# Routed-expert stage of a four-layer block: the normalisation of groups 2 to 7 moves from VectorE to ScalarE, and the last statistics move around the first group

## The chip, the cores and the metric

The kernel runs on one core of one Trainium2 chip. The metric is the device time of one execution in microseconds. A core has a matrix engine (TensorE, PE in the profile), VectorE (DVE), ScalarE (ACT), GpSimd (POOL) and SyncE (SP), which run their own instruction streams and meet at semaphores. An engine takes its own instructions strictly in the order in which they are written.

## The reference, cut to what matters

Eight residual sublayers run one after the other on x of 16 x 256 tokens by 128 features, in float32. Before each stands a layer norm of every token. The fourth is a routed mixture of 16 small experts with the best four chosen per token:

```python
def _layernorm(x, axis=-1, eps=1e-05):
    m = jnp.mean(x, axis=axis, keepdims=True)
    v = jnp.var(x, axis=axis, keepdims=True)
    return (x - m) / jnp.sqrt(v + eps)

def _L1_ffn_ref(x, expert_sel, keys, values, route_scale):     # 16 experts of width 32, K = 4
    sel_probs = jax.nn.sigmoid(jnp.einsum('btd,ed->bte', x, expert_sel))
    _, sel_index = jax.lax.top_k(sel_probs, K)
    sel_val = jnp.take_along_axis(sel_probs, sel_index, axis=-1)
    sel_val = sel_val / jnp.clip(sel_val.sum(-1, keepdims=True), 1e-09) * route_scale
    scores_all = jax.nn.relu(jnp.einsum('btd,edh->bteh', x, keys))
    values_all = jnp.einsum('bteh,ehv->btev', scores_all, values)
    selected = jnp.take_along_axis(values_all, sel_index[..., None], axis=2)
    return (selected * sel_val[..., None]).sum(axis=2)

x = x + _L0_xattn_ref(...); x = x + _L0_ffn_ref(...)
x = x + _L1_xattn_ref(_layernorm(x), ...)      # attention "a1"
x = x + _L1_ffn_ref(_layernorm(x), ...)        # routed experts "f1": the changed stage
x = x + _L2_xattn_ref(...); x = x + _L2_ffn_ref(...); x = x + _L3_xattn_ref(...); x = x + _L3_ffn_ref(...)
```

## The kernel before

**Layout.** X stays in on-chip memory for the whole kernel, as 32 tiles of 128 tokens by 128 features. Four tiles are a group, so there are 8 groups. The sublayers are named a0, f0, a1, f1, a2, f2, a3, f3. There is no scheduler and no planner: each engine has one function per sublayer, and the order of the work on an engine is the order of the Python code, written by hand. Semaphores counted from the start of the kernel tie the engines together.

**The layer norm** is made in pieces. When a residual has been added to a group (residual, L295), VectorE takes the statistics of its four tiles (BN_STATS, L302). Mean and variance are worked out for a stretch of tiles at once: ln_var_dve is six small VectorE operations (L217 to L225), ln_finish_act is two on ScalarE, Ln and Exp, which give one over the root of the variance (L255, L257), and ln_rstd_dve is four on VectorE (L236 to L242). For f1 the tiles are in two parts, tiles 0 to 23 (part 0, groups 0 to 5) and tiles 24 to 31 (part 1, groups 6 and 7): EARLY is 24. Part 0 is done inside the attention a1. Then a group is normalised into hrow, one of two buffers, in four operations of 128x128, by VectorE (normalise, L271, subtract and multiply) or by ScalarE (normalise_act, L264, Identity with scale and bias). TensorE turns the four tiles by transposes (turn, L282), and ScalarE copies the result into hT (take_turned, L287).

**The stage f1** handles group g in body(g, ...) on TensorE, ScalarE and VectorE. On TensorE body g does, in this order:

- turn(g+1), which waits until group g+1 is normalised;
- for g from 1 to 6 a piece of the next attention a2: its keys K (L471, which for g = 2, 3 and 4 wait for VectorE's operations on the piece before), then its values V (L339);
- keys(0), keys(1) (L1518), tr(0) (L1525), keys(2), tr(1), the routing logits of group g+1 (L1471), val(0) (L1535), keys(3), tr(2), val(1), tr(3), val(2), val(3).

Here keys(t) multiplies tile t by all experts' keys, tr(t) transposes the hidden values, and val(t) multiplies them by the values. Between them VectorE makes hidden(t) (L1639, relu times gate) and ScalarE hidT(t) (L1600, the copy of the transposed hidden values, for which val(t) waits). In the words below, hidT(t) is ScalarE's operation L1600 for tile t. VectorE's body g does hidden(0), hidden(1), the residual of group g-1, hidden(2), hidden(3), the gates of group g+1 (f1_gates, L1484 to L1501), **the normalisation of group g+2 (L271)**, and then small pieces for a2: masks at g = 0 (L770), keys_cos at g = 1 (L748), keys_sin at g = 2 (L754 to L759), keys16 and keys_cos at g = 3 (L765, L748), keys_sin at g = 4, keys16 at g = 5. At g = 0 the whole finish of part 1 (L217 to L242, with ScalarE's L255 and L257 in the middle) stands between the gates and the normalisation. VectorE starts the stage with `dve.sem_inc(S("f1_hid"), 2)` (L1632), for which TensorE's keys(0) of group 0 waits.

Of the kernel before, what the change touches and what calls it, by code (L numbers as in the profile page):

```python
# [30 lines left out]
N_GROUPS = N_TILES // 4  # L31
# [40 lines left out]
def build(nc, dram):  # L72
    with ExitStack() as ctx:
# [66 lines left out]
        def bank(i):  # L140
            return psum[:, i, :]
# [25 lines left out]
        EARLY = 24  # L167
# [7 lines left out]
        def ln_parts(s):  # L175
            return LN_PARTS.get(s, ((0, N_TILES),))
# [8 lines left out]
        def sem(s, name):  # L185
            return S("all_" + name)

        def at(s, name):
            return sum(count(x, name) for x in SUB[:SUB.index(s)])
# [55 lines left out]
        def ln_finish_dve(dve, s, k=0):  # L245
            ln_var_dve(dve, s, k)
            ln_rstd_dve(dve, s, k)

        def ln_finish_act(act, s, k=0):

            lo, hi = ln_parts(s)[k]
            if s in ("a0", "a1") and k == 0:
                act.preload_act_table_set("natural_log_exp_and_others")
            act.wait_ge(sem(s, "var"), at(s, "var") + k + 1)
            act.activation(lnw[:, 5, lo:hi], lnw[:, 4, lo:hi], ACT.Ln).then_inc(S("all_lnv"), 1)  # L255
            act.wait_ge(S("all_lnv"), at(s, "var") + k + 1)
            act.activation(lnw[:, 6, lo:hi], lnw[:, 5, lo:hi], ACT.Exp, scale=-0.5).then_inc(sem(s, "std"), 1)  # L257

        def normalise_act(act, s, g, j, k=0):
            act.wait_ge(sem(s, "ln"), at(s, "ln") + LN_STEPS * (k + 1))  # L260
            act.wait_ge(sem(s, "normed"), at(s, "normed") + g)
            act.wait_ge(sem(s, "turned"), at(s, "turned") + g + 1)
            for t in range(GT):
                ins = act.activation(hrow[:, j, t * P:(t + 1) * P], tile_of(X, 4 * g + t), ACT.Identity,  # L264
                                     scale=rstd[:, ds(4 * g + t, 1)], bias=shifted[:, ds(4 * g + t, 1)])
            ins.then_inc(sem(s, "normed"), 1)

        def normalise(dve, s, g, j):
            dve.wait_ge(sem(s, "turned"), at(s, "turned") + g + 1)
            for t in range(GT):  # L270
                ins = dve.tensor_scalar(hrow[:, j, t * P:(t + 1) * P], tile_of(X, 4 * g + t),  # L271
                                        mean[:, ds(4 * g + t, 1)], rstd[:, ds(4 * g + t, 1)],
                                        ALU.subtract, ALU.mult)
            ins.then_inc(sem(s, "normed"), 1)
# [32 lines left out]
        def stats_done(dve, s, nxt, k=0):  # L307
            dve.wait_ge(sem(s, "bn"), at(s, "bn") + ln_parts(nxt)[k][1])
            dve.sem_inc(sem(nxt, "stats"), 1)
# [489 lines left out]
        def heads_dve(dve, L, o, nxt):  # L799
            s = L.s  # L800
            early = nxt.early
            mx, norm, res = o.mx, o.norm, o.res
            for b in range(B + 2):
                if b + 2 < B:
                    mx(b + 2, 0)
                    mx(b + 2, 1)
                if b == 1:
                    ln_rstd_dve(dve, s, 1)
                if 1 <= b <= B:
                    norm(b - 1)  # L810
                if b == B - 2 and early:
                    ln_rstd_dve(dve, nxt.s, 0)
                    normalise(dve, nxt.s, 0, 0)
                if b == B and early:
                    nxt.gates0(dve)
                if b >= 2 and b % 2:
                    res((b - 3) // 2)
                if b == B - 3 and early:
                    stats_done(dve, s, nxt.s, 0)
                    ln_var_dve(dve, nxt.s, 0)  # L820
            stats_done(dve, s, nxt.s, int(early))

# [630 lines left out]
        f1 = Carve()  # L1455
# [19 lines left out]
        def f1_exps(act, g, j):  # L1475

            act.wait_ge(S("f1_lg"), g + 1)
            act.activation(prob1[j], bank(1)[:, 0:GT * MOE1_E], ACT.Exp, scale=-1.0).then_inc(S("f1_ex"), 1)
# [111 lines left out]
        def f1_act(act, a2):  # L1590
            act.sem_inc(S("f1_hidT"), 2)

            def body(g, j, last):
                if not last:
                    take_turned(act, "f1", g + 1, 1 - j)
                for t in range(GT):
                    act.wait_ge(S("f1_tr"), 4 * g + t + 1)
                    if t >= 2:
                        act.wait_ge(S("f1_val"), 4 * g + t - 1)
                    act.activation(hidT1[t % 2], bank(4 + t % 2), ACT.Copy).then_inc(S("f1_hidT"), 1)  # L1600
                    if t == 1 and not last:
                        f1_exps(act, g + 1, 1 - j)
                    if t == 1 and last:
                        take_turned(act, "a2", 0, 0)
                    if t >= 2 and last:
                        a2.takeQ(t - 2)
                    if t == 0 and g in (5, 6):
                        a2.values(2 * g - 10, 6)
                    if t == 0 and last:
                        normalise_act(act, "a2", 1, 1)  # L1610
                if g == 3:
                    a2.keys16(0)
                if g == 5:
                    a2.values(1, 6)
                    a2.keys16(1)
                    ln_finish_act(act, "a2", 0)
                if g == 6:
                    a2.values(3, 6)
                    normalise_act(act, "a2", 0, 0)

            for g in range(N_GROUPS):
                body(g, g % 2, g == N_GROUPS - 1)
                if g == 0:
                    ln_finish_act(act, "f1", 1)
            a2.rotated16(0)
            a2.rotated16(1)
            take_turned(act, "a2", 1, 1)
            a2.takeN(0)

        def f1_dve(dve, a2):  # L1630
            s = "f1"
            dve.sem_inc(S("f1_hid"), 2)  # L1632
            ga = gate1.rearrange("p (t e) -> p t e", t=GT)

            def hidden(g, t):
                dve.wait_ge(S("f1_h_ps"), 4 * g + t + 1)
                if t >= 2:
                    dve.wait_ge(S("f1_tr"), 4 * g + t - 1)
                dve.scalar_tensor_tensor(out=hid1[t % 2].rearrange("p (e h) -> p e h", h=MOE1_H),  # L1639
                                         in0=bank(2 + t % 2).rearrange("p (e h) -> p e h", h=MOE1_H), scalar=0.0,  # L1640
                                         in1=ga[:, t, :].unsqueeze(2).to_broadcast([P, MOE1_E, MOE1_H]),
                                         op0=ALU.max, op1=ALU.mult).then_inc(S("f1_hid"), 1)

            def res(g):
                residual(dve, s, g, bank(7), False, (S("f1_val"), 4 * g + 4))

            def body(g, j):
                fixed = isinstance(g, int)
                hidden(g, 0)
                hidden(g, 1)  # L1650
                if not (fixed and g == 0):
                    res(g - 1)
                if g == 5:
                    stats_done(dve, s, "a2", 0)
                    ln_var_dve(dve, "a2", 0)
                if g == 6:
                    ln_rstd_dve(dve, "a2", 0)
                hidden(g, 2)
                hidden(g, 3)
                if not (fixed and g == N_GROUPS - 1):  # L1660
                    f1_gates(dve, g + 1, 1 - j)
                if fixed and g == 0:
                    ln_finish_dve(dve, s, 1)
                if not (fixed and g >= N_GROUPS - 2):
                    normalise(dve, s, g + 2, j)
                if g == 0:
                    a2.masks()
                if g == 1:
                    a2.keys_cos(0, 6)
                if g == 2:  # L1670
                    a2.keys_sin(0, 6)
                if g == 3:
                    a2.keys16(0)
                    a2.keys_cos(1, 6)
                if g == 4:
                    a2.keys_sin(1, 6)
                if g == 5:
                    a2.keys16(1)

            for g in range(N_GROUPS):  # L1680
                body(g, g % 2)
            res(N_GROUPS - 1)
            stats_done(dve, s, "a2", 1)
            ln_var_dve(dve, "a2", 1)
            for b in range(2):
                a2.mx(b, 0)
                a2.mx(b, 1)
# [851 lines left out]
```

## Time and profile before

| | us |
|---|---|
| median of 3 runs | 1238.36 |
| lowest and highest run | 1228.98 and 1240.29 |
| the profiled execution, its own time | 1236.59 |
| its span, first to last instruction | 1234.8 |
| the stage f1 in it, TensorE's first keys to its last val | 368.5 to 473.3 |

The times of single instructions come from the one profiled execution. Its own time is 1.8 us over its span, and 1.8 us under the median of the runs. The stage f1 is about 105 us of the 1235, so 8.5%.

### The profile page before, as it was taken

To read this page: it belongs to the slowest core of one execution; us is meant where nothing else is said; L and a number is where in the kernel's file an instruction comes from. 1 tells how busy PE (TensorE), PEld (TensorE's weight loads), DVE (VectorE), ACT (ScalarE), POOL (GpSimd) and SP (SyncE) were. 2 spreads that over 40 slices of the span, in tenths; PEclk is the share of its full clock that TensorE was granted. 3 is DMA by queue.
4 is the path that set the end of the run, shared out by engine and by line. 5 is a ranking of instruction groups with operands and counts; after the bars stand their busy time and mean duration, and the time that the engine had idled before them with its cause. 6 is when DMAs were issued, how large, how long until landed. Compare 5 with 4: busy or idle time off the path is not lost.

```text
span 1234.8 us, 21182 instructions
## 1 busy us (share of the span) xinstructions
PE 1019.8 (83%) x7331; PEld 656.3 (53%) x7331; DVE 906.6 (73%) x2297; ACT 634.7 (51%) x1007; POOL 354.4 (29%) x334
## 2 busy tenths in 40 slices
PE   5868800679978997899669999998889979999998
PEld 3653300655546674454326667666645546666665
DVE  4685699858885674577678898999568876666666
ACT  3424578856632244565267777775466533333332
POOL 5600000002110003345098999995112200000000
PEclk9988965779999997999759999999989999999999
DMA  7000000010000000000000000000000000000000
GB/s 272 1 1 1 1 0 0 1 65 2 1 2 1 1 1 1 2 1 2 1 0 1 1 0 0 0 1 1 1 1 2 2 1 10 9 8 8 8 9 18
DMA packets 8959, 13.51 MB, mean 11 GB/s; under 512 B 816, under 2 KB 6704, under 8 KB 8624
## 3 DMA queue, kind: packets, MB, share of 16 engines
q1 hardware_dynamic: 8880, 12.46, 2.9%
q8 instruction: 50, 0.82, 0.3%
q14 instruction: 29, 0.24, 0.1%
HBM read 10.36 MB, written 2.10 MB: 10 GB/s over the span
## 4 chain that ended last, share of the span: by engine, by line
PE 43%; DVE 26%; issue 7%; ACT 4%; DVEq 0%; ACTq 0%
DVE big L785 7%; DVE hq L780 7%; PE psum L558 5%; PE psum L2216 5%; PE psum L2199 5%; PE psum L2202 5%; PE psum L1518 2%; DVE big L2041 2%; PE psum L1762 2%; PE psum L1770 2%; PE psum L512 2%; DVE big L789 2%; ACT psum L1879 2%; PE psum L1777 2%; PE psum L1773 2%
## 5 line engine op out<-in xcount | busy, mean ns | idle before, releaser
L780 DVE TENSOR_REDUCE hq<-psum 128x16 f32<-128x1024 f32 x96 | 114.3, 1221 | 82.7 <-PE psum L512 42.8
L1951 POOL TENSOR_TENSOR big<-big 128x512 f32<-128x512 f32 x128 | 128.6, 1043 | 21.4 <-ACT big L1856 21.4
L2249 ACT ACTIVATE big<-psum 128x512 f32<-128x512 f32 x80 | 47.7, 598 | 141.1 <-PE psum L2199 141.0
L422 POOL TENSOR_TENSOR big<-big,w_const 128x256 f32<-128x256 f32 x48 | 35.8, 748 | 260.3 <-PE psum L558 227.3
L1879 ACT ACTIVATE psum<-big,tmp 128x512 f32<-128x512 f32 x128 | 85.0, 687 | 25.0 <-DVE big L2041 22.3
L2041 DVE SCALAR_TENSOR_TENSOR big<-big,tmp,psum 128x512 f32<-128x512 f32 x128 | 90.4, 744 | 4.8 <-ACT psum L1879 1.9
L2270 DVE TENSOR_TENSOR big<-big,psum 128x512 f32<-128x512 f32 x80 | 54.4, 687 | 51.1 <-PE psum L2202 49.7
L668 ACT ACTIVATE big<-psum 128x1024 f32<-128x1024 f32 x64 | 62.0, 1021 | 55.1 <-PE psum L542 55.1
L785 DVE RECIPROCAL big<-psum 128x256 f32<-128x256 f32 x48 | 84.0, 1750 | 7.7 <-PE psum L558 7.6
L2216 PEld LDWEIGHTS psum<-tmp,big 128*128 128x128 f32 x512 | 66.7, 192 | 41.5 <-issue 38.0
L2279 DVE SCALAR_TENSOR_TENSOR X<-psum,big,X 128x128 f32 (+1 forms) x256 | 72.3, 344 | 17.9 <-PE psum L2216 15.5
L2202 PE MATMUL psum<-hT,tmp 128*128 128x512 f32 x160 | 81.8, 593 | 2.7 <-DVEq L2260 2.7
L1961 POOL TENSOR_TENSOR big<-big 128x1024 f32<-128x1024 f32 x32 | 75.2, 2360 | 26.3 <-DVE big L2041 26.3
L2199 PE MATMUL psum<-hT,tmp 128*128 128x512 f32 x160 | 82.5, 597 | 0.0
L1432 PE MATMUL psum<-f_downT,tmp 128*128 128x128 f32 x192 | 25.8, 301 | 68.0 <-DVE tmp L1315 68.0
L287 ACT ACTIVATE hT<-psum 128x512 f32<-128x512 f32 x64 | 38.1, 595 | 76.8 <-PE psum L282 76.8
L558 PE MATMUL psum<-big 128*32 128x256 f32 x768 | 53.1, 393 | 28.2 <-DVE big L789 28.2
L2216 PE MATMUL psum<-tmp,big 128*128 128x128 f32 x512 | 68.2, 276 | 8.5 <-DVE big L2270 8.5
L1201 DVE TENSOR_REDUCE amax<-big 128x1 f32<-128x1536 f32 x32 | 55.9, 1749 | 22.6 <-ACT big L1341 22.6
L282 PE MATMUL psum<-w_const,hrow 128*128 128x128 f32 x256 | 44.4, 301 | 33.8 <-DVE hrow L1225 10.9
L538 PE MATMUL psum<-hq,big 32*128 32x256 f32 x768 | 65.6, 428 | 6.9 <-DVE hq L780 6.6
L1801 PEld LDWEIGHTS psum<-w_const,big 128*128 128x128 f32 x512 | 61.0, 192 | 8.6 <-issue 8.6
(243 smaller groups left out, 2353.5 us busy)
## 6 DMA issues: line engine op xcount, KB each, us to landing
out<-X SPq DMA_DIRECT2D x8, 256.0 KB, 2.3
tmp<-in_pack_f SPq DMA_DIRECT2D x1, 1924.0 KB, 7.4
w_f<-in_pack_f SPq DMA_DIRECT2D x1, 1280.0 KB, 12.2
tmp<-in_pack_once SPq DMA_DIRECT2D x1, 960.0 KB, 7.1
X<-in_x SPq DMA_DIRECT2D x1, 768.0 KB, 5.3
w_a<-in_pack_a SPq DMA_DIRECT2D x3, 256.0 KB, 7.5
w_a<-in_pack_a SPq DMA_DIRECT2D x1, 704.0 KB, 9.6
w_f<-in_pack_f SPq DMA_DIRECT2D x1, 576.0 KB, 5.0
```

Source lines behind the costliest of these rows:

```text
L538: pe.matmul(bank(1 + r)[:, 256 * e:256 * e + 256], L.kbd[rows, b, e * P:(e + 1) * P], L.qT[b % L.ahead][rows, :], start=True, stop=False)
L558: ins = pe.matmul(bank(6)[32 * r:32 * r + 32, 256 * which:256 * which + 256], w, L.pt[b % 2][:, (2 * r + e) * 256:(2 * r + e + 1) * 256], ...
L780: dve.tensor_reduce(nm, psum[:, 1 + 2 * t:3 + 2 * t, :].rearrange("p c (r l k) -> p (c r) l k", r=2, k=SK), AX.X, ALU.max, negate=True).th ...
L785: dve.reciprocal(L.rz, bank(6)[:, 256:512]).then_inc(hs("rz"), 1)
L1879: act.activation(bank(EX_BANK + h % 2), ssum[t][:, h * 512:(h + 1) * 512], ACT.Exp, bias=shift2[:, t * NH2 + h:t * NH2 + h + 1]).then_inc( ...
L1951: ins = pool.tensor_tensor(ssum[t][:, h * 512:(h + 1) * 512].rearrange("p (i j) -> p i j", i=ROWS2), st[:, 0, h, 0:ROWS2].unsqueeze(2).to_ ...
L1961: pool.tensor_tensor(ew[t][:, 0:left], ew[t][:, 0:left], ew[t][:, NFOLD * 512:], ALU.add)\
L2041: dve.scalar_tensor_tensor(out=ew[t][:, blk], in0=ssum[t][:, blk], scalar=best2[:, t, h, 7:8], in1=bank(EX_BANK + h % 2), op0=ALU.is_ge, o ...
L2199: pe.matmul(bank(1 + e % 2), W["f3_w1"][:, e * P:(e + 1) * P], hT[:, j, :], start=True, stop=True)\
L2202: pe.matmul(bank(3 + e % 2), W["f3_w3"][:, e * P:(e + 1) * P], hT[:, j, :], start=True, stop=True)\
L2216: ins = pe.matmul(bk[:, t * P:(t + 1) * P], hid3[e % 2][:, t * P:(t + 1) * P], W["f3_w2"][:, e * P:(e + 1) * P], start=True, stop=True) \
L2279: dve.scalar_tensor_tensor(out=xt, in0=bank(5 + e % 2)[:, t * P:(t + 1) * P], scalar=gate3[:, t * E3 + e:t * E3 + e + 1], in1=xt, op0=ALU. ...
```

## The change

Three pieces of code move. ScalarE normalises groups 2 to 7 (normalise_act), after hidT(2) and ahead of hidT(3) of body g = 0 to 5, where VectorE did it at the end of the same body. The six operations ln_var_dve of part 1 move from the end of VectorE's body 0 to the end of attention a1, ahead of VectorE's start of the stage; ScalarE's Ln and Exp of part 1 move ahead of its body 0; and the four operations ln_rstd_dve go between hidden(1) and hidden(2) of body 0.

```diff
@@ heads_dve, the attention's VectorE function, at its end
             stats_done(dve, s, nxt.s, int(early))
+            if nxt.s == "f1":
+                ln_var_dve(dve, nxt.s, 1)
@@ f1_act, body(g, j, last), in the loop over t
                     if t == 1 and not last:
                         f1_exps(act, g + 1, 1 - j)
+                    if t == 2 and g + 2 < N_GROUPS:
+                        normalise_act(act, "f1", g + 2, j, int(4 * (g + 2) >= EARLY))
@@ f1_act
+            ln_finish_act(act, "f1", 1)
             for g in range(N_GROUPS):
                 body(g, g % 2, g == N_GROUPS - 1)
-                if g == 0:
-                    ln_finish_act(act, "f1", 1)
@@ f1_dve, body(g, j)
                 hidden(g, 0)
                 hidden(g, 1)
-                if not (fixed and g == 0):
+                if g == 0:
+                    ln_rstd_dve(dve, s, 1)
+                else:
                     res(g - 1)
@@ f1_dve, body(g, j)
                 if not (fixed and g == N_GROUPS - 1):
                     f1_gates(dve, g + 1, 1 - j)
-                if fixed and g == 0:
-                    ln_finish_dve(dve, s, 1)
-                if not (fixed and g >= N_GROUPS - 2):
-                    normalise(dve, s, g + 2, j)
```

ScalarE from the start of the stage to the copy at the start of body 1, before. The operand names are tensors: big holds the stage's work tiles, lnw the layer norm's small values; what stands in brackets are the semaphores that a row waits for.

```order
L1478 ACTIVATE big<-psum 128x64 [waits f1_lg]
L287 ACTIVATE hT<-psum 128x512 [waits all_turned]
L1600 ACTIVATE big<-psum 128x512 [waits f1_tr] x2
L1478 ACTIVATE big<-psum 128x64 [waits f1_lg]
L1600 ACTIVATE big<-psum 128x512 [waits f1_val,f1_tr] x2
L255 ACTIVATE lnw<-lnw 128x8 [waits all_var]
L257 ACTIVATE lnw<-lnw 128x8 [waits all_lnv]
L287 ACTIVATE hT<-psum 128x512 [waits all_turned]
```

The same stretch of ScalarE in the changed kernel, where the hidT rows have line 1602 and the gates' exponential has line 1480.

```order
L1480 ACTIVATE big<-psum 128x64 [waits f1_lg]
L255 ACTIVATE lnw<-lnw 128x8 [waits all_var]
L257 ACTIVATE lnw<-lnw 128x8 [waits all_lnv]
L287 ACTIVATE hT<-psum 128x512 [waits all_turned]
L1602 ACTIVATE big<-psum 128x512 [waits f1_tr] x2
L1480 ACTIVATE big<-psum 128x64 [waits f1_lg]
L1602 ACTIVATE big<-psum 128x512 [waits f1_val,f1_tr]
L264 ACTIVATE hrow<-X,lnw 128x128 [waits all_turned,all_normed,all_ln]
L264 ACTIVATE hrow<-X,lnw 128x128 x3
L1602 ACTIVATE big<-psum 128x512 [waits f1_val,f1_tr]
L287 ACTIVATE hT<-psum 128x512 [waits all_turned]
```

The four L264 rows now split the pair hidT(2), hidT(3), and the two small operations stand ahead of the copy that was first.

VectorE at the end of its body 0, before: from the last operation of the gates to the normalisation of group 2.

```order
L1501 SCALAR_TENSOR_TENSOR big<-big,rscale 128x64
L217 TENSOR_TENSOR lnw<-stats 128x8
L218 SCALAR_TENSOR_TENSOR lnw<-stats 128x8
L219 TENSOR_TENSOR lnw<-stats 128x8
L221 SCALAR_TENSOR_TENSOR lnw<-lnw 128x8
L223 TENSOR_SCALAR lnw<-lnw 128x8
L225 SCALAR_TENSOR_TENSOR lnw<-lnw 128x8
L236 TENSOR_TENSOR lnw<-lnw 128x8
L238 SCALAR_TENSOR_TENSOR lnw<-lnw 128x8
L240 SCALAR_TENSOR_TENSOR lnw<-lnw 128x8
L242 SCALAR_TENSOR_TENSOR lnw<-lnw 128x8
L271 TENSOR_SCALAR hrow<-X,lnw 128x128 x4
```

VectorE in the changed kernel, from the last statistics of a1 to the end of hidden(1) and what follows it (the hidden rows have line 1642 now).

```order
L302 BN_STATS stats<-X 128x6 x4
L217 TENSOR_TENSOR lnw<-stats 128x8
L218 SCALAR_TENSOR_TENSOR lnw<-stats 128x8
L219 TENSOR_TENSOR lnw<-stats 128x8
L221 SCALAR_TENSOR_TENSOR lnw<-lnw 128x8
L223 TENSOR_SCALAR lnw<-lnw 128x8
L225 SCALAR_TENSOR_TENSOR lnw<-lnw 128x8
L1642 SCALAR_TENSOR_TENSOR big<-psum,big 128x512 x2
L236 TENSOR_TENSOR lnw<-lnw 128x8
L238 SCALAR_TENSOR_TENSOR lnw<-lnw 128x8
L240 SCALAR_TENSOR_TENSOR lnw<-lnw 128x8
L242 SCALAR_TENSOR_TENSOR lnw<-lnw 128x8
```

Six of the ten small rows stand ahead of hidden(0) now and four between hidden(1) and hidden(2), and the L271 row is gone.

## Rows read from the trace of the kernel before

**Rows 1.** The page of the profile, part 1: busy time of each engine.

```profile
PE 1019.8 (83%) x7331; PEld 656.3 (53%) x7331; DVE 906.6 (73%) x2297; ACT 634.7 (51%) x1007; POOL 354.4 (29%) x334
```

**Rows 2.** Who waited for whom, TensorE, 366 to 480 us: total, times, longest.

```profile
PE psum L282 <- DVE hrow L271: 5.2, 5, 2.6
PE psum L471 <- DVE big L748: 1.2, 1, 1.2
...
PE psum L1525 <- DVE big L1639: 0.2, 1, 0.2
```

**Rows 3.** Timeline, end of body 2: start, length, instructions, [idle before <-releaser].

```profile
404.63 0.69 DVE L1639 SCALAR_TENSOR_TENSOR big<-psum,big 128x512 f32<-128x512 f32 x1 [1.82 <-PE psum L1518]
...
405.06 0.60 ACT L1600 ACTIVATE big<-psum 128x512 f32<-128x512 f32 x1 [2.06 <-PE psum L1525]
...
406.19 2.01 PE L1535 MATMUL psum<-w_f,big 128*128 128x128 f32 x16
406.39 0.60 ACT L1600 ACTIVATE big<-psum 128x512 f32<-128x512 f32 x1 [0.73 <-PE psum L1525]
...
407.67 1.11 DVE L271 TENSOR_SCALAR hrow<-X,lnw 128x128 f32<-128x128 f32 x4
...
408.83 0.66 PE L282 MATMUL psum<-w_const,hrow 128*128 128x128 f32 x4 [0.63 <-DVE hrow L271]
```

**Rows 4.** Timelines of TensorE, VectorE and ScalarE, body 0 and start of body 1.

```profile
368.52 3.21 PE L1518 MATMUL psum<-w_f,hT 128*128 128x512 f32 x4 [2.96 <-DVEq L1632]
...
373.53 0.69 DVE L1639 SCALAR_TENSOR_TENSOR big<-psum,big 128x512 f32<-128x512 f32 x1 [1.06 <-PE psum L1518]
...
377.05 0.60 ACT L1600 ACTIVATE big<-psum 128x512 f32<-128x512 f32 x1 [2.06 <-PE psum L1525]
...
379.65 0.17 DVE L217 TENSOR_TENSOR lnw<-stats 128x8 f32<-128x8 f32 x1
...
380.10 0.16 DVE L225 SCALAR_TENSOR_TENSOR lnw<-lnw 128x8 f32<-128x8 f32 x1
...
380.78 0.17 DVE L236 TENSOR_TENSOR lnw<-lnw 128x8 f32<-128x8 f32 x1 [0.51 <-ACT lnw L257]
...
381.65 1.11 DVE L271 TENSOR_SCALAR hrow<-X,lnw 128x128 f32<-128x128 f32 x4
...
382.82 1.11 PE L282 MATMUL psum<-w_const,hrow 128*128 128x128 f32 x4 [2.64 <-DVE hrow L271]
```

**Rows 5.** Chain of waits by start and length: where bodies 1, 2 and 4 run.

```profile
392.27 0.69 DVE big L1639
...
396.48 0.66 PE psum L282 x4
...
397.14 1.13 PE psum L471 x2
...
432.20 0.69 DVE big L1639
```

**Rows 6.** Timeline, the step from body 3 to body 4.

```profile
421.25 1.28 DVE L765 TENSOR_SCALAR big<-big,w_const 128x2048 bf16<-128x2048 f32 x1
...
422.44 0.74 DVE L748 SCALAR_TENSOR_TENSOR big<-psum,w_const,w_a 128x512 f32<-128x512 f32 x1
423.24 1.61 PE L471 MATMUL psum<-ctx,w_a 128*128 128x512 f32 x2 [1.20 <-DVE big L748]
```

**Rows 7.** Busy time by stretch; behind the engines, PEclk, the granted TensorE clock.

```profile
384.00:386.00 2.00, 2.00 (x3) 0.74 (x3) 0.00 (x0) 0.57 (x1) 0.00 (x0) 0.50 0.00 0
...
424.00:425.00 1.00, 1.00 (x2) 0.47 (x2) 0.00 (x0) 0.00 (x0) 0.00 (x0) 0.50 0.00 0
```

**Rows 8.** Timeline, ScalarE normalising a group of a2, and its next operation.

```profile
465.08 1.64 ACT L264 ACTIVATE hrow<-X,lnw 128x128 f32<-128x128 f32 x4
...
466.62 0.58 ACT L1600 ACTIVATE big<-psum 128x512 f32<-128x512 f32 x1
```

**Rows 9.** Timeline, TensorE's turn of group 7 at the start of body 6.

```profile
449.33 0.60 PE L282 MATMUL psum<-w_const,hrow 128*128 128x128 f32 x4
```

## The prediction

> **What bounds the kernel now.** The page gives TensorE 83% and VectorE 73% of the span [rows 1]; that is an average over eight sublayers, and the change touches one of them, so I read that stage by itself. The stage is 105 us of the span, and a change of order inside it can hardly move the whole by 1%, which is about 12 us and about what a measurement of this kernel can tell from no change (its three runs lie 11 us apart).
>
> I read TensorE's waits in the stage first. It waited five times for VectorE's normalisation, 5.2 us in all, the longest 2.6, and once 1.2 us for VectorE's keys_cos [rows 2]. The rest of the stage TensorE works through, or waits for its own chain. Then I read the timeline of one body that repeats [rows 3]. The reader is to see a fork behind keys(3). VectorE does hidden(3) at 404.63, the gates, and the normalisation of group 4 at 407.67. Beside it ScalarE does hidT(2) at 405.06 and hidT(3) at 406.39, and TensorE val(2) and val(3) from 406.19 to 408.20. The two arms meet at turn(4), at 408.83, and VectorE's arm is later by 0.63. So the normalisation is on the path, but only by its last 0.63 us; behind that stands val(3).
>
> Third, the clock. Where the wait was long, TensorE then ran at the lower of its levels: a granted clock of 0.50, which is 1.2 GHz, stands at 384 to 386 after the wait of 2.64, and at 424 to 425 after the waits of 0.64 and 1.20 that came 0.66 us apart [rows 4, 6, 7]. After the single wait of 0.63, turn(4) took 0.66 as it does at 2.4 GHz, against 1.11 after the long one [rows 3, 4].
>
> **Edit 1: the six operations ahead of the stage.** Their span is from 379.65 to 380.26, 0.61 us [rows 4]. In their new place they stand ahead of the semaphore step L1632, and TensorE's first keys waited for exactly that step, after 2.96 us of idleness [rows 4]. So the whole **0.6 us is lost** there. TensorE ran slow there already (3.21 us for four), so the longer wait adds no second price. GpSimd has nothing to do at that point, so nothing should stretch the operations. ScalarE's Ln and Exp come before its copy of the turned group 1, which is then later too; that copy is first used by the logits of group 1, behind tr(1), and ScalarE has nothing else to do until hidT(0), so this costs nothing. If that cover were gone it would cost the two operations, under 0.5 us, as the step from 380.26 to 380.78 shows [rows 4].
>
> **Edit 2: the four operations between hidden(1) and hidden(2).** They take from 380.78 to 381.65, 0.87 us. VectorE waited 1.06 us for TensorE ahead of hidden(2) [rows 4], so they fit, with 0.2 us to spare. Cost 0; between 0 and 0.2.
>
> **Edit 3: what goes from the end of VectorE's body 0.** From 379.65 to 381.65 the finish of part 1 took 2.0 us, then the normalisation 1.1, and turn(2) began at 382.82 [rows 4].
>
> **Edit 4: ScalarE's normalisation.** Four such operations occupy ScalarE for 465.08 to 466.62, 1.54 us until its next can start (1.64 by their own length) [rows 8]. They stand between hidT(2) and hidT(3). hidT(3) started 0.73 us after hidT(2) ended [rows 3], so it is held back: hidT(2) ends at 405.66, the normalisation at 407.20, hidT(3) at 407.80 instead of 406.99. val(3), half of the 2.01 us of the two, could start at 407.2 before and starts at 407.85 now; it ends at about 408.85, and turn(4) follows it at once. Before, turn(4) started at 408.83. **The wait of 0.63 for VectorE is gone and one of about 0.65 for ScalarE stands in its place.** The worth of this handover is 0. It is one of five such, and each comes out its own way:
>
> - Into body 1: all of body 0 is 0.6 later (edit 1). hidT(2) then ends at 378.25, the normalisation at 379.8, hidT(3) at 380.4, val(3) at 381.4, and turn(2) starts there and not at 382.82: **1.4 us gained**, with the loss of edit 1 taken off already. The wait of 2.64 shrinks to one of about 0.7, so I take the clock to stay up. Body 1 took 9.45 us from turn(2) to its hidden(3) at 392.27; body 2, with the same work, took 8.15, from 396.48 to 404.63 [rows 3, 4, 5]. **1.3 us gained** by the clock.
> - Into bodies 2, 3 and 5: 0 each, as worked out, by 0.2 either way. In body 3 VectorE's keys_sin made tr(0) wait 0.2 us for hidden(0), the one wait of TensorE's L1525 [rows 2], and VectorE is now 1.1 earlier: **0.2 gained**.
> - Into body 4: TensorE waits twice, 0.64 for turn(5), which is replaced as above, and then 1.20 for keys_cos, which follows keys16 on VectorE [rows 6]. VectorE reaches both 1.12 us earlier without its normalisation, so keys_cos ends at about 422.1 and not at 423.2, just behind turn(5): **1.1 gained**. With the long wait goes the slow stretch: from K at 423.24 to hidden(3) at 432.20 are 8.96 us, the same stretch of body 2, from 397.14 to 404.63, is 7.49 [rows 3, 5, 6]. **1.5 gained.**
> - Into body 6: turn(7) had no wait [rows 9]; the values of a2 fill TensorE there, and they cover ScalarE's 1.54 too: 0. Group 7 is the last that is moved.
>
> **The sum**: 1.4 + 1.3 + 0.2 + 1.1 + 1.5 = 5.5 us, of which 2.7 are waits and 2.8 the clock. The profiled execution would go from 1236.59 to 1231.1, and the median, 1.8 above it, from 1238.36 to **1232.9 us**. Nothing behind the stage should take it back: attention a2 waits for the stage's last residual, not for a transfer.
>
> A rule speaks against the change. Four normalising operations take VectorE 1.11 us and ScalarE 1.64 [rows 3, 8]. The Trainium skill, page "ScalarE: Activation LUTs", section "Rules for kernel authors", says to use VectorE and not ScalarE for additions and multiplications, because VectorE is the faster one per element. The trace agrees on the durations; whether they reach the end is the question of the third rival, where the rule would give 1241.0 in place of 1232.9.
>
> **The rivals.**
>
> 1. *The waits go, the clock does not come back.* The clock falls in the same two bodies after the shorter waits, or one fall goes and another comes elsewhere in the kernel, since every later wait now lies differently. For it: turn(5) shows that two short waits near each other were enough. Against: the single waits of 0.63 ahead of turn(3), turn(4) and turn(6) never were. Gain 2.7 us, **1235.7**.
> 2. *The middle handovers gain as well.* If hidT(3) could run in time, up to 0.6 us would come at each of four handovers, 2.5 us more than the forecast: **1230.4**. Against: ScalarE takes its work in order, and 1.54 is longer than the 0.73 that was free.
> 3. *ScalarE becomes the bound, by its slower operations.* If turn waited for them as it did for VectorE's, from the same start, each of five handovers on the path would cost 1.64 - 1.11 = 0.53 us, 2.6 in all, **1241.0**, slower. It decides on where they start: they must end later than VectorE's did. Against: they start at 405.66, not at 407.67 as VectorE's [rows 3]. This is what the rule of the Trainium skill, page "ScalarE: Activation LUTs", would make of it.
> 4. *The wait for hidT(3) costs the clock.* The new wait of 0.65 stands between val(2) and val(3), at the handovers into bodies 1 to 5. If the clock fell at each of the five, where it fell at two before, three more falls of 1.4 us against 2.7 us of waits give +1.5 us: **1239.9**, slower. The point from which it decides lies between one wait of 0.64, after which the clock stood, and 0.64 with 1.20 behind it, after which it fell.
> 5. *It does not do what it says.* VectorE's arm is replaced by something equally late everywhere, also in body 0: **1238.4**.
>
> **How the numbers follow.** The forecast has 0.52, rival 1 0.22, rival 2 0.08, rival 3 0.03, rival 4 0.08, rival 5 0.07. All of them lie between 1230 and 1241. What the range must add is the scatter of the runs: single runs lie from 9.4 below their median to 1.9 above it, and the medians of two kernels can differ by some 5 us for that alone. I give 1225 to 1241. Faster by over 1% (under 1226) is only to be had by that scatter on top of the gain: 0.06. Slower by over 1% would need an effect that no row shows: 0.03. Within 1%: 0.91.
>
> **What the profile after would show.** If edit 1 is right, the first keys start at about 369.1. If edit 4 is right, turn(2) has no wait for a normalisation and starts at about 381.4 to 381.5; in bodies 1 to 4 TensorE waits about 0.65 us for ScalarE's L1602 between val(2) and val(3), and the distance from one hidden(3) to the next stays at 12.4 in the plain bodies. K in body 4 follows turn(5) within 0.3 us, and the granted clock is 1.00 from there on and in body 1. No activation table is loaded in the stage. The stage's last residual comes 5 to 6 us earlier. The prediction is wrong in its mechanism if turn waits for L264, if hidT(3) is not held back, or if the clock falls in the plain bodies; and in its size if the clock falls in body 1 or 4 all the same.

## The result, and the profile after

The changed kernel takes **1229.2 us** (median of 20 runs, 1225.9 to 1233.3), the kernel before 1238.1 (20 runs, 1229.0 to 1240.7). The ratio is 0.9932, 95% interval 0.9922 to 0.9942: 8.4 us faster by the ratio, 7.2 to 9.7 by its interval, and 0.7%, so within 1%. The forecast was 1232.9 with a range of 1225 to 1241.

Single executions of one kernel differ by several microseconds, and the medians of a few runs by one or two, so the traces are compared by the stage alone: from the start of the last residual of a1 to the start of the stage's own last residual (both L295 on VectorE). Before, that was 366.70 to 473.36, 106.66 us. After:

```profile
367.88 0.69 DVE L295 TENSOR_TENSOR X<-X,psum 128x512 f32<-128x512 f32 x1
```

```profile
467.19 0.70 DVE X L295
```

The first row is of the timeline, the second of the chain of waits. The stage takes 99.31 us, **7.35 us less**. The page of the changed kernel shows the move of 24 small operations from VectorE to ScalarE, and shares that hardly differ from [rows 1]:

```profile
PE 1017.8 (83%) x7331; PEld 655.1 (53%) x7331; DVE 900.3 (73%) x2273; ACT 643.2 (52%) x1031; POOL 354.2 (29%) x334
```

Who TensorE waited for in the stage (total, times, longest) answers to [rows 2]. No turn waits any more; val(3) waits for ScalarE's hidT(3) five times, and K of body 4 waits 0.34 and not 1.20:

```profile
PE psum L1520 <- DVEq L1635: 3.4, 1, 3.4
PE psum L1537 <- ACT big L1602: 2.4, 5, 0.5
...
PE psum L471 <- DVE big L748: 0.3, 1, 0.3
```

The timeline at the end of body 2 answers to [rows 3]. ScalarE's four operations stand between hidT(2) and hidT(3), which starts 2.03 us behind hidT(2) and not 1.33; the 2.01 us block of val(2) and val(3) is split by a wait of 0.47, and turn(4) follows without one:

```profile
402.01 0.69 DVE L1642 SCALAR_TENSOR_TENSOR big<-psum,big 128x512 f32<-128x512 f32 x1 [1.82 <-PE psum L1520]
...
402.45 0.60 ACT L1602 ACTIVATE big<-psum 128x512 f32<-128x512 f32 x1 [2.06 <-PE psum L1527]
...
402.94 1.64 ACT L264 ACTIVATE hrow<-X,lnw 128x128 f32<-128x128 f32 x4
...
403.58 1.06 PE L1537 MATMUL psum<-w_f,big 128*128 128x128 f32 x8
...
404.48 0.58 ACT L1602 ACTIVATE big<-psum 128x512 f32<-128x512 f32 x1
...
405.11 1.16 PE L1537 MATMUL psum<-w_f,big 128*128 128x128 f32 x8 [0.47 <-ACT big L1602]
...
406.11 0.60 PE L282 MATMUL psum<-w_const,hrow 128*128 128x128 f32 x4
...
406.54 1.02 PE L471 MATMUL psum<-ctx,w_a 128*128 128x512 f32 x2
```

The start of the stage and of body 1 answers to [rows 4]:

```profile
370.17 3.47 PE L1520 MATMUL psum<-w_f,hT 128*128 128x512 f32 x4 [3.42 <-DVEq L1635]
...
378.27 0.69 DVE L1642 SCALAR_TENSOR_TENSOR big<-psum,big 128x512 f32<-128x512 f32 x1 [2.33 <-PE psum L1520]
...
382.36 0.60 PE L282 MATMUL psum<-w_const,hrow 128*128 128x128 f32 x4
```

The first keys wait 3.42 us, 0.46 more than before, and take 3.47 and not 3.21. From the last residual of a1 to turn(2) are 14.48 us, before 16.12. The granted clock, by stretch as in [rows 7], is 1.00 in body 1 and at the start of body 4, where it was 0.50:

```profile
384.00:386.00 2.00, 2.00 (x9) 0.92 (x8) 1.11 (x2) 0.00 (x0) 0.00 (x0) 1.00 0.00 0
418.00:420.00 2.00, 1.66 (x8) 0.94 (x7) 0.83 (x2) 1.27 (x2) 0.00 (x0) 1.00 0.00 0
```

A table of the stage by its bodies, from one hidden(3) to the next (starts of L1639, in the changed kernel L1642), says where the 7.35 us are, beside what the prediction had:

| stretch | before | after | gained | predicted |
|---|---|---|---|---|
| last residual of a1 to hidden(3) of body 0 | 9.91 | 10.39 | -0.48 | -0.6 |
| to turn(2) | 6.21 | 4.09 | 2.12 | 2.0 |
| turn(2) to hidden(3) of body 1 | 9.45 | 7.74 | 1.71 | 1.3 |
| body 2 | 12.36 | 11.91 | 0.45 | 0 |
| body 3 | 12.54 | 11.84 | 0.70 | 0.2 |
| body 4 | 15.03 | 12.52 | 2.51 | 2.6 |
| body 5 | 12.54 | 12.19 | 0.35 | 0 |
| to the stage's last residual | 28.62 | 28.63 | 0 | 0 |
| sum | 106.66 | 99.31 | 7.35 | 5.5 |

### The profile page after: what moved, and what is told of

It is laid out like the page before. It is cut to its first block, busy times and chain, and to the rows that moved or that the text cites. A ratio compares the mean times of both kernels' runs of the same rounds, so it can differ in the third digit from the quotient of the medians.

```text
span 1228.2 us, 21187 instructions
## 1 busy us (share of the span) xinstructions
PE 1017.8 (83%) x7331; PEld 655.1 (53%) x7331; DVE 900.3 (73%) x2273; ACT 643.2 (52%) x1031; POOL 354.2 (29%) x334
## 4 chain that ended last, share of the span: by engine, by line
PE 44%; DVE 24%; issue 7%; ACT 4%; DVEq 0%; ACTq 0%
DVE big L785 7%; DVE hq L780 7%; PE psum L558 5%; PE psum L2203 5%; PE psum L2200 5%; PE psum L2217 5%; PE psum L1520 2%; DVE big L2042 2%; PE psum L1763 2%; PE psum L1771 2%; PE psum L512 2%; PE psum L1774 2%; PE psum L1537 2%; PE psum L1778 2%; DVE big L789 2%
## 5 line engine op out<-in xcount | busy, mean ns | idle before, releaser
L282 PE MATMUL psum<-w_const,hrow 128*128 128x128 f32 x256 | 43.4, 297 | 28.9 <-DVE hrow L1227 11.4
```

## The experiments

Ten new kernels ran, and each of the two once more. All diffs are against the kernel named with them. The stage's time below is always from the last residual of a1 to its own last residual.

**Is the stage's time a property of the kernel?** The two kernels once more, unchanged, for a second trace each.

> The kernel before once more, unchanged, for a second trace of it: is the stage's time the same in another execution? From the last residual of a1 to its own last residual it took 106.66 us. Both theories rest on that: if it repeats within 0.3 us, differences of stages are differences of kernels, and what single executions differ by lies outside it. Rival: the clock falls at other bodies in another execution, and the stage differs by 1.5 us or more.

> The changed kernel once more, unchanged. The stage took 99.31 us. Expected: 99.3 again, with the rest of the kernel anywhere within 1124 and 1135 us, as in the nine traces so far. Rival: the new wait of 0.47 or the 0.34 ahead of K lets the clock fall in some executions, and the stage comes out 1.4 us or more longer.

Measured: 366.03 to 472.69, **106.66 us**, and 367.55 to 466.86, **99.31 us**, each the same to 0.01 us, with the same waits, and with falls of the clock at the same places (before: at the start, in body 1 and in body 4; after: at the start alone). What is left of the two executions is 1129.2 and 1130.7 us. So a difference of 0.1 us between two stages can be read. A difference of some microseconds between two whole executions can't be put down to the stage. The rivals fell.

**One part of the change at a time.** First ScalarE's normalisation alone, against the kernel before:

```diff
@@ f1_act, body
+                    if t == 2 and g + 2 < N_GROUPS:
+                        normalise_act(act, "f1", g + 2, j, int(4 * (g + 2) >= EARLY))
@@ f1_dve, body
-                if not (fixed and g >= N_GROUPS - 2):
-                    normalise(dve, s, g + 2, j)
```

> ScalarE normalises groups 2 to 7 as in the changed kernel; the statistics of part 1 stay where they were, at the end of VectorE's body 0. Handover theory: turn(2) needs group 2, which is part 0, so it never needed those ten operations; once ScalarE normalises, they are off the path, and moving them ahead of the stage only delays the first keys by 0.5 us. So this kernel is 0.5 us faster than the changed one, about 1228.7, and TensorE's first wait is 2.9 and not 3.4 us. Rival, statistics theory: the 2.0 us that left the tail of VectorE's body 0 are what body 1 gained (with the clock 3 us); then this kernel is 3 us slower than the changed one, about 1232.

Measured: 1230.3 us (ratio 0.9937, 0.9912 to 0.9962); the stage takes **98.83 us**, 0.48 less than the changed kernel's, by exactly what the start of the stage lost. The statistics theory fell: once ScalarE normalises, the ten operations at the end of body 0 are waited for by nobody, and moving them costs. The whole kernel's median does not show this half microsecond: about 1228.7 was expected, and the ratio is the changed kernel's within its interval. TensorE's first wait is 2.96 again:

```profile
367.61 3.19 PE L1518 MATMUL psum<-w_f,hT 128*128 128x512 f32 x4 [2.96 <-DVEq L1634]
```

Then the statistics alone (the changed kernel with normalise back on VectorE, behind the gates):

> Only the statistics of part 1 move as in the changed kernel; VectorE normalises all groups as before. Handover theory: turn(2) waits for VectorE's chain without the 2.0 us of the finish, about 0.7 in place of 2.64; the first keys lose 0.5; the clock stays up in body 1, 1.5 us more. About 3 us faster than before, 1235.1; the wait for keys_cos in body 4 stays at 1.2 and the clock falls there. Rival: the clock falls in body 1 all the same, then only 1.5 us, 1236.6.

Measured: 1232.6 us (ratio 0.9974, 0.9955 to 0.9994); the stage takes **103.53 us**, 3.13 less than before. turn(2) waits 0.63 in place of 2.64, as the total of five turns shows, and the clock stays up in body 1, while K of body 4 waits 1.2 as ever (waits, then a stretch behind turn(2)):

```profile
PE psum L1520 <- DVEq L1633: 3.4, 1, 3.4
PE psum L282 <- DVE hrow L271: 3.2, 5, 0.6
PE psum L471 <- DVE big L748: 1.2, 1, 1.2
```

```profile
382.00:384.00 2.00, 2.00 (x7) 0.75 (x6) 0.76 (x2) 0.00 (x0) 0.00 (x0) 1.00 0.00 0
```

The parts don't add: 7.83 and 3.13 us alone, 7.35 together. They cure the same wait of 2.64, and the second then only costs 0.48.

**Only two of the six groups.** ScalarE normalises groups 2 and 5, VectorE the others, statistics as before:

```diff
@@ f1_act, body
+                    if t == 2 and g in (0, 3):
+                        normalise_act(act, "f1", g + 2, j, int(4 * (g + 2) >= EARLY))
@@ f1_dve, body
-                if not (fixed and g >= N_GROUPS - 2):
+                if g in (1, 2, 4, 5):
                     normalise(dve, s, g + 2, j)
```

> ScalarE normalises only groups 2 and 5 (bodies 0 and 3), the two whose handovers had the long waits; VectorE the other four; statistics where they were. Handover theory: all of the gain of bodies 1 and 4, waits and clock, is in these two, and the other handovers stay at 12.36 and 12.54: the stage takes 98.8 + 3 x 0.45 + 0.25 = 100.4 us, so three quarters of the gain come from two groups. Rival: the gain is spread evenly over the six groups, and the stage takes about 104.

Measured: the stage takes **100.30 us**, where 100.4 was expected: 6.36 of the 7.83 us of all six groups. The handovers into bodies 1 and 4 carry the change, because there VectorE had other work in the same chain (the finish of part 1, keys16 with keys_cos), and because each took a fall of the clock with it.

**What are the 0.45 us of a plain body?** The prediction had 0 there. In this kernel VectorE gets its time back to spend, in the place of its normalisation; ScalarE normalises as in the changed kernel:

```diff
@@ f1_dve, body, of the changed kernel
                     f1_gates(dve, g + 1, 1 - j)
+                if g < N_GROUPS - 2:
+                    for x in range(3):
+                        dve.wait_ge(S("spare"), 3 * g + x)
+                        dve.tensor_scalar(spare[:, :], tile_of(X, 4 * (g + 2) + x), mean[:, ds(x, 1)],
+                                          rstd[:, ds(x, 1)], ALU.subtract, ALU.mult).then_inc(S("spare"), 1)
```

> The changed kernel with three operations on VectorE, each waiting for the one before, in the place that its normalisation had (same operation and shape, written to a spare tile that nobody reads): about 1.1 us of VectorE's time in each of bodies 0 to 5, for which no turn waits. Piece theory: in the kernel before, K stood behind VectorE's normalisation too, through keys_cos and keys_sin, which read the bank that K writes; that is the 0.45 us per plain body that the sum had at 0. So here the plain bodies 2, 3 and 5 lose 0.2 to 0.4 us each against the changed kernel, body 4 loses 1.1, and the stage takes 101.0 to 101.5, or 102.5 to 103 if the clock falls in body 4. Rival: only the place of the wait counts (turn against val(3)), K never mattered, plain bodies stay at 11.9 and 11.84.

Measured: the stage takes **101.83 us**, between the two ranges that were given: the clock did not fall in body 4, but bodies 2 and 3 lost 0.45 and 0.70 and not 0.2 to 0.4. Bodies 2, 3 and 5 take 12.36, 12.54 and 12.54 us, to the hundredth what they took before the change, although no turn waits for VectorE. The timeline at the end of body 2 shows what does (line numbers are one higher here; L283 is turn, L472 K, L755 keys_sin):

```profile
404.44 1.11 DVE L1671 TENSOR_SCALAR spare<-X,lnw 128x128 f32<-128x128 f32 x3
404.50 1.16 PE L1538 MATMUL psum<-w_f,big 128*128 128x128 f32 x8 [0.48 <-ACT big L1603]
405.47 0.74 DVE L755 SCALAR_TENSOR_TENSOR big<-psum,w_const,w_a 128x512 f32<-128x512 f32 x1
405.49 0.60 PE L283 MATMUL psum<-w_const,hrow 128*128 128x128 f32 x4
...
406.26 1.12 PE L472 MATMUL psum<-ctx,w_a 128*128 128x512 f32 x2 [0.17 <-DVE big L755]
```

K writes the bank that keys_cos and keys_sin read, so it waits for them. They stand behind VectorE's normalisation, and here they are 0.17 us late even behind a turn that itself waited for nothing. Body 2 has the same wait for keys_cos (0.18), and in body 5, which has no K, the values V wait 0.17 for keys_sin. Without the extra work K follows turn at once (406.54 behind 406.11 in the changed kernel). In the kernel before, the same dependence shows only in the row of K's weight load (PEld):

```profile
408.69 0.74 DVE L754 SCALAR_TENSOR_TENSOR big<-psum,w_const,w_a 128x512 f32<-128x512 f32 x1
...
409.49 0.30 PEld L471 LDWEIGHTS psum<-ctx,w_a 128*128 128x128 f32 x2 [0.24 <-DVE big L754]
```

From hidden(3) to K are 4.86 us there (404.63 to 409.49) and 4.86 here (401.40 to 406.26), though turn starts 0.11 us earlier here. In body 4 the wait for VectorE is 1.37 here:

```profile
420.00 1.12 PE L472 MATMUL psum<-ctx,w_a 128*128 128x512 f32 x2 [1.37 <-DVE big L749]
```

Body 4 takes 13.55 us, 1.03 more than in the changed kernel, and body 1, where nothing of VectorE stands ahead of K, 11.84 and loses nothing. So the gain of the plain bodies is VectorE's 1.1 us of free time, by way of K or V and, in body 3, of hidden(0); the wait at the turn itself was only changed for another. The place theory fell.

**Where ScalarE does it.** The changed kernel with the call one step later, `t == 3`, behind hidT(3):

> The changed kernel with ScalarE's normalisation one step later, behind hidT(3) (t == 3). Handover theory: val(3) is no longer held, and turn waits for ScalarE's L264 in its stead: hidT(3) ends 2.35 us behind the start of hidT(2), the normalisation 1.64 later; turn starts 0.2 us earlier than it did behind VectorE's, with the slow start behind a wait, so a plain body takes 12.1 to 12.2 us against 11.9 of the changed kernel and 12.36 before; the stage about 100.5. Rival, place does not matter: the same four operations on the same engine, the same 99.3.

Measured: the stage takes **99.55 us**, 0.95 less than expected. val(3) is not held, and turn waits 0.37 or 0.38 us for L264, six times:

```profile
PE psum L282 <- ACT hrow L264: 2.2, 6, 0.4
```

Bodies 2 and 3 take 11.83 and 11.75 us, even 0.08 and 0.09 less than the changed kernel's; the expectation of 12.1 lacked the same piece as the prediction, K. The place costs in body 6, where turn(7) waited for nobody and now waits 0.38: from hidden(3) of body 5 to that of body 6 are 13.28 us against 12.70.

The changed kernel with the call one step earlier, `t == 1`, behind the exponential of the gates, where ScalarE stood idle for 2.06 us ahead of hidT(2):

> The changed kernel with ScalarE's normalisation one step earlier, behind the exponential of the gates (t == 1), ahead of hidT(2). ScalarE stands idle there for 2.06 us and the four operations take 1.54. Handover theory: hidT(3) is in time, val(3) follows val(2) without the wait of 0.47, and without the slow start behind a wait (1.16 against 0.9 us); 0.7 us less at each of five handovers, 3.3 in all, about 1225.9. Rival: something else is next at once (turn's copy, or hidT(2) is late), and the kernel stays within 1 us of the changed one, 1229.

Measured: 1228.8 us (ratio 0.9926, 0.9901 to 0.9951); the stage takes **97.05 us**, 2.26 less than the changed kernel, of 3.3 expected. TensorE waits neither for hidT(3) nor at a turn, and bodies 2 and 5 take 11.33 and 11.52. Body 3 gains 0.32 only, since tr(0) waits 0.19 for VectorE's hidden(0) again, and body 4 keeps its 12.52, since the wait for keys_cos takes the whole gain back:

```profile
PE psum L471 <- DVE big L748: 1.0, 1, 1.0
```

With the statistics where they were besides:

> The normalisation one step earlier as in the run before this one, and the statistics where they were before the change. Handover theory: both gains add, 3.3 and 0.5 us on the changed kernel, about 1225.4. Rival, statistics theory: VectorE's ten operations at the end of body 0 delay something of body 1, and the kernel is not faster than the one with the statistics moved.

Measured: 1227.2 us (ratio 0.9925, 0.9900 to 0.9949); the stage takes **96.57 us**, again 0.48 less. The medians (1225.9 and 1225.4 were expected for the two) don't tell these kernels apart.

**How long a wait can be before it costs the clock.** The changed kernel with two more operations ahead of each group's normalisation:

```diff
@@ f1_act, body, of the changed kernel
                     if t == 2 and g + 2 < N_GROUPS:
+                        for x in range(2):
+                            act.wait_ge(S("spare"), 2 * g + x)
+                            act.activation(spare[:, :], tile_of(X, 4 * (g + 2) + x), ACT.Identity,
+                                           scale=rstd[:, ds(x, 1)], bias=shifted[:, ds(x, 1)]).then_inc(S("spare"), 1)
                         normalise_act(act, "f1", g + 2, j, int(4 * (g + 2) >= EARLY))
```

> The changed kernel with two more operations of the normalisation's size on ScalarE ahead of each group's normalisation (they write to a spare tile; each waits for the one before). Handover theory: hidT(3) is held 1.0 us longer, TensorE waits 1.5 and not 0.47 us between val(2) and val(3), and each of five handovers is 1.0 longer, body 4 0.7 by the wait for keys_cos that it hides: the stage goes from 99.3 to 104. Clock rival (number 4 of the prediction): a wait of 1.5 in each body is enough to bring the granted clock to 0.50, and another 1.4 us per fall is lost, up to 111. If the clock holds, the point from which that rival decides lies above 1.5 us.

Measured: the stage takes **103.69 us**, 4.38 more, with five waits of 1.39 us and one of 0.21 (sum of the six, here L1538 for L1603):

```profile
PE psum L1538 <- ACT big L1603: 7.2, 6, 1.4
```

The granted clock is 1.00 in every stretch from 376 to 438. Bodies 1, 2, 3 and 5 are longer by 0.91 to 0.93 us, as their waits are. Body 4 is longer by 0.30 only, and not by the 0.7 expected: its 0.34 ahead of K went, and with it the slower start behind that wait. Body 6, for which nothing was expected, lost 0.41, with the sixth wait. Nothing was lost to the clock. So rival 4 of the prediction does not come true at waits of 0.47, nor at 1.39.

**The best version.** On top of the earlier call and the statistics in their old place, keys_cos ahead of keys16 on VectorE in body 3:

```diff
@@ f1_dve, body
                 if g == 3:
-                    a2.keys16(0)
                     a2.keys_cos(1, 6)
+                    a2.keys16(0)
```

> The best version so far (ScalarE's normalisation ahead of hidT(2), statistics where they were), with keys_cos ahead of keys16 on VectorE in body 3, so that K of body 4 waits for one operation less (1.28 us). With ScalarE's normalisation out of the way this wait of 1.03 us is TensorE's longest in the stage. Handover theory: it goes whole, and with it the slow start behind it; the stage from the last residual of a1 to its own last residual goes from 96.6 to 95.4 us, the kernel to about 1226. Rival: turn, or VectorE's hidden(0) of body 4 behind the later keys16, takes its place, and the stage stays within 0.4 us of 96.6.

Measured: 1226.0 us (ratio 0.9896, 0.9880 to 0.9913); the stage takes **95.30 us**. Body 4 goes from 12.52 to 11.25 us, and K waits for nobody. That is 1.27 us for a wait of 1.03: the slower start behind a wait went too.

On top of that, the step that releases the first keys, moved ahead of a1's last residual:

```diff
@@ heads_dve, at b == B
                     nxt.gates0(dve)
+                    if nxt.s == "f1":
+                        dve.sem_inc(S("f1_hid"), 2)
@@ f1_dve
-            dve.sem_inc(S("f1_hid"), 2)
```

> The version with keys_cos first, and VectorE's semaphore step that releases the first keys moved ahead of the last residual and its statistics of a1 (the banks that keys(0) and keys(1) write are free by then). The step is the longest wait left in the stage, 2.96 us, and TensorE runs at 0.50 behind it. Handover theory: keys(0) and keys(1) run in that gap, hidden(0) starts right behind the statistics, 1.7 us earlier, and with the clock up hidden(3) of body 0 comes 2.8 us earlier: stage 92.5 in place of 95.3, the kernel about 1223. Rival: the clock falls all the same, because TensorE now waits for hidden(0), and only 1.7 us come.

Measured: **1223.1 us** (ratio 0.9882, 0.9863 to 0.9901); the stage takes **92.54 us**. The keys start ahead of the residual and take 1.98 us, where they took 3.21 before (timeline):

```profile
365.86 1.98 PE L1520 MATMUL psum<-w_f,hT 128*128 128x512 f32 x4 [1.22 <-DVEq L817]
365.98 0.69 DVE L295 TENSOR_TENSOR X<-X,psum 128x512 f32<-128x512 f32 x1 [0.23 <-DVE big L1503]
...
367.73 1.29 DVE L1642 SCALAR_TENSOR_TENSOR big<-psum,big 128x512 f32<-128x512 f32 x2 [0.15 <-DVE stats L302]
...
368.48 0.66 PE L1527 MATMUL psum<-w_const,big 128*128 128x128 f32 x4 [0.63 <-DVE big L1642]
```

The granted clock is 1.00 from 362 to 462 us, so the rival fell. The residual itself now waits 0.23 us (second row), and a1 is 0.21 us longer up to it, so 2.55 of the 2.76 us are left. It is the fastest kernel of this study by the stage, and 1.2% under the kernel before by its five runs; the interval of the version before it overlaps with its own. It does without one half of the change, the moved statistics.

## Why the prediction was right, and where it was not

**Direction and place: right.** Hidden(3) of body 0 comes 0.48 us later (predicted 0.6). The words "no second price" did not quite hold: the first four keys took 0.26 us longer and hidden(0) came 0.73 later (4.09 us behind the residual, before 3.36), but a quarter of a microsecond of it was won back by hidden(3). Edit 2 cost nothing: hidden(2) of body 0 follows without a new wait of TensorE. The two handovers with long waits give 2.12 - 0.48 + 1.71 and 2.51 us, 5.9 of the 7.35, where the prediction had 5.3; the kernel with these two groups alone confirms it. The clock came back in both bodies, so rival 1 did not happen in the stage; for its falls elsewhere see the last paragraph of this section. K in body 4 follows turn(5) with a wait of 0.34, where 0.3 was expected.

**The handover at turn: right.** The prediction said that a wait of 0.65 for ScalarE takes the place of 0.63 for VectorE. Measured: 0.47 and then a slower start of val(3), 1.16 against 1.06 us. From the start of val(2) to the start of turn(4) were 2.64 us [rows 3], and are 2.53. Rival 3 fell with it, and with it the rule of the Trainium skill, page "ScalarE: Activation LUTs", section "Rules for kernel authors", as a forecast for this case: the durations point the way the page has it (1.64 us on ScalarE against 1.11 on VectorE), yet the slower engine makes a faster kernel, since what counts is whose queue is free at that point.

**The step that failed** is "Into bodies 2, 3 and 5: 0 each": the three gave 0.45, 0.50 beside the 0.2 foreseen, and 0.35. The sum counted VectorE's freed 1.1 us only where a wait for VectorE stood in the list of waits: at turn, at the K of body 4 and at one tr(0). It missed the K of bodies 2 and 3 and the V of body 5, which were bound by VectorE too and showed only as a late weight load behind a late turn. K started 0.66 us behind turn(3) and turn(4) there. Where turn had waited as well but K did not depend on VectorE's normalisation, it started 0.49 behind it: in body 1 with only the statistics moved (380.66 to 381.15), and in body 3 with the normalisation behind hidT(3) (403.66 to 404.15). The kernel with VectorE kept busy shows it by giving all of it back. The prediction's sign "the distance stays at 12.4" was wrong for the same reason: it went to 11.91 and 11.84. In body 1, too, the stretch behind turn(2) gained 1.71 and not 1.3: body 2, which was taken as its measure, had the cost of K in it.

**Beyond the stage** the prediction had no gain and no loss. In two traces of each kernel the rest takes 1129.9 and 1129.2 us before, 1131.0 and 1130.7 after. The medians of the runs, less the stage, are 1131.5 and 1129.9. So 7.35 us are shown to be the stage's; the further 1.1 of the ratio's 8.4 lie inside its interval, and whether they are real stays open. The median came out 3.7 us under the forecast: 1.9 of it is the stage (7.35 for the 5.5 of the sum), the other 1.8 lies outside the stage or in the scatter of the medians. The stage's 7.35 alone would have given 1231.0, so the range did not hold by luck.

The rest is not the same in the two kernels. From the stage's last residual to the next one, the first of a2, are 49.86 and 49.85 us in the two traces before, and 46.89 in both after. By the granted clock of each 2 us, it stood at 0.50 for some 20 us of that stretch before and for some 10 after. The second ten microseconds behind the stage's last residual, before and after (columns as in [rows 7]):

```profile
483.36:493.36 10.00, 7.39 (x39) 4.29 (x40) 0.71 (x1) 4.43 (x10) 6.17 (x8) 0.50 0.00 1
477.19:487.19 10.00, 6.84 (x46) 3.72 (x46) 1.78 (x2) 6.18 (x15) 6.12 (x8) 0.83 0.00 0
```

Two other places take it back: the last two residuals of f2 lie 30.5 us apart before and 33.5 after, and 2.4 us more stand ahead of the stage, between 245 and 291 us, where nothing was changed. So falls of the clock did go in one place and come in another, as the second half of rival 1 had it, but outside the stage. The ten other kernels have 43.4 to 50.0 us in the first of these stretches, and no experiment shows what decides it; that it is the change's doing is not shown.

## What to carry to other kernels

An operation that leaves an engine frees everything that stood behind it in that engine's order. List all consumers of the operations behind it, those too whose wait is hidden because something else is as late, and price each; the list of waits names only who came last. When a wait has two arms that end within a few tenths of a microsecond, taking work from one and putting it in the other changes the name of the wait and not its length, unless it goes where that engine stands idle: here one step earlier, ahead of hidT(2), was worth another 2.3 us. And a part that was meant to shorten the same wait should be tried again without its companion: the moved statistics cost 0.5 us once ScalarE normalised.

## What the runs showed of the hardware that was not expected

- The stage repeats to 0.01 us between executions (106.66 twice, 99.31 twice), while the rest of the kernel, whose instructions no experiment but the last touched, took between 1124.0 and 1134.8 us in the traces of this study. The rest is not noisy everywhere either: a1, from its first residual to its last, took 76.75 to 76.77 us in every trace but the last kernel's. What differs are a few stretches in which the clock is at 0.50 for a longer or shorter time. The 20 runs of the changed kernel say the same: the mean granted clock was 0.930 in the fastest (1225.9 us) and 0.918 in the slowest (1233.3). With hardly any noise in a stage, one trace of each kernel settles an effect of 0.1 us in it that 20 timed runs could not.
- In this stage the granted clock fell behind every single wait of TensorE of 2.64 us and more (2.64, 2.96, 3.42). Below that the length of a wait alone did not tell. It fell to 0.50 behind 0.64 and 1.20 us with 0.66 us of work between them (in both traces before, and with only the statistics moved), and it stayed at 1.00 behind single waits of 1.39, five times, and behind 0.48 and 1.37 us with 1.6 us of work between them, and behind 1.22 and 0.63 with 2.0 between them (the last kernel). The clock of the stretch at K behind the 1.37, in the kernel with VectorE kept busy:

```profile
420.00:422.00 2.00, 2.00 (x5) 1.04 (x6) 0.00 (x0) 0.00 (x0) 0.00 (x0) 1.00 0.00 0
```

- A fall of the clock costs about 1.5 us, and two kernels give it without anything else in it. Behind turn(2), with the same work and VectorE normalising in both, body 1 took 9.45 us before and 7.80 with only the statistics moved, where the clock stayed up: 1.65 us. From K to hidden(3) of body 4 were 8.96 us before and are 7.49 with VectorE kept busy: 1.47 us. The prediction had 1.3 and 1.5.
